# Stage 1 of an attention and feed-forward block: one chunk's statistics ahead, the largest latents read from the values, and an earlier start of TensorE

## The chip, the core and the metric

The kernel runs on one core of a Trainium2 chip. The metric is device time in microseconds from the first to the last instruction of one launch, with the launch's own edges. All data starts and ends in HBM. TensorE has two clock levels, 1.2 and 2.4 GHz, granted by the chip.

## The reference

x is 2 x 2048 tokens of 1024 numbers, in f32. The block computes:

```
n    = layernorm(x)                                # no learned scale
Cq   = n @ Wq_d + bq_d                             # 1024 -> 12
Ckv  = n @ Wkv_d + bkv_d                           # 1024 -> 4, the "latents"
q    = Cq @ W_qk + b_qk                            # 32 heads of 4
p    = softmax(q . Ckv / 2)                        # 32 heads, 2048 x 2048 per batch
V    = Ckv @ Wv_u + bv_u                           # 32 heads of 32
x    = x + (p @ V) @ Wo + bo
x    = x + layernorm(x) @ W.T + bias + the sum over 8 low-rank updates (lora_A, lora_B, lora_weights)
```

Keys and values of all heads are made from the same four latents of a token. So a head's product with the values needs the four latents and a column of ones only, and Wv_u, Wo and the biases are folded into one matrix beforehand.

## The kernel before

The 4096 tokens are 8 chunks of 512 (`CHUNKS`, N = 512), four to a batch (`CB`). Each chunk is four tiles of 128 tokens (`TT`). The code is written out by hand: every engine has its own program, and semaphores are the only thing between them. An engine runs its program strictly in that order, so a wait holds up all that stands behind it.

**Stage 1** makes queries, keys and values of all 8 chunks. For chunk c:
- SyncE loads four tiles of x, 512 KB each (L332), into a ring of four places (`y`, `xn` and two parts of `area`). A place is loaded anew when its chunk has been turned and measured.
- VectorE measures it: `statistics`, eight BATCH_NORM_STATS2 (L1124) and four aggregates (L1201). GpSimd makes 1/sqrt(variance + eps) of it in 14 small operations on 4 columns (L490 to L501) and a diagonal matrix `diag` (L505); TensorE multiplies `diag` with ones (`spread_r`, L705), and ScalarE moves the product to `o_sb` (`move_r`, L590).
- TensorE turns x with the identity, eight `turn_x` of four 128x128 transposes (L678; `turn_first`, L685, for the first half of chunk 0). ScalarE moves each to `x_turned` (`move_turned`, L556). Two `down` (L698) of 32 columns multiply it with `w_down`. The second of chunk c stands in the next chunk's stretch, behind its second `turn_x`.
- VectorE multiplies the result with `o_sb` (`scale_parts`, L1211, into `down_part`). TensorE sums the parts (`sum_parts`, L711), which gives the latents, and makes the queries of `down_part` (`queries`, L727). ScalarE moves the latents twice (`move_latents` L561, `round_latents` L565), TensorE turns them (`turn_latents`, L722), and ScalarE moves these to `c_wide` (`move_values`, L570).
- VectorE takes the largest latent of the chunk (L1225, `c_max`) and splits the latents in bf16 parts, the keys (`split_latents`, L1227 to L1231, into `key_t`). GpSimd splits the queries (`split_q`, L513 to L517), and SyncE stores them (`store_q`, L342, six transfers a chunk, out of two places in turn; `move_q` of chunk c + 2 waits for the store of chunk c).

VectorE's order is: statistics of chunks 0 and 1, then for c from 1 on `scale_parts(c - 1)`, `split_latents(c - 2)`, `statistics(c + 2)`, with `statistics(2)` and `statistics(3)` both behind `scale_parts(0)`.

**The decision.** The softmax has no maximum of its own per row if a bound on the scores is small. Per batch, the largest latents (L735, L1240) weigh the absolute queries (`bounds`, L743); VectorE takes the largest of the result (L1165), TensorE turns it (L792), and VectorE writes `tight` (L1248, L1250). TensorE, ScalarE and SyncE read `tight` and branch; with these inputs the bound is tight and a long part is skipped. The bound also gives a shift that is stored with the queries (`split_shift`, `store_shifts` L362); the first block of queries is then loaded (L369). TensorE runs `keep_busy` beside its waits: transposes whose result nobody reads (L775).

**Stage 2** starts behind it: TensorE makes scores (L903), ScalarE takes 2048 exponentials of 128x1024 (L634), TensorE multiplies them with the values (L914), and the preparation of the weights and the dense layer stand between.

Of the kernel before, what the change touches and what calls it, by code (L numbers as in the profile page):

```python
# [21 lines left out]
F32 = mybir.dt.float32  # L22
# [11 lines left out]
def build_block(nc, x, wq_d, bq_d, w_qk, b_qk, wkv_d, bkv_d, wv_u, bv_u, wo, bo,  # L34
# [38 lines left out]
    with ExitStack() as ctx:  # L73
# [55 lines left out]
        lat = nc.alloc_sbuf_tensor_at("lat", [P, 2, N], F32, offset=probs_at)  # L129
        down_part = nc.alloc_sbuf_tensor_at("down_part", [P, N], F32, offset=probs_at + 4 * 2 * N)  # L130
        part_b = nc.alloc_sbuf_tensor_at("part_b", [P, N], BF16, offset=probs_at + 4 * 3 * N)
        part_high = nc.alloc_sbuf_tensor_at("part_high", [P, 2, N], BF16, offset=probs_at + 4 * 4 * N)
# [13 lines left out]
        c_max = sb("c_max", [P, CHUNKS], F32)  # L146
        c_maxb = sb("c_maxb", [P, B], F32)
# [27 lines left out]
        w_in = sem("w_in")  # L175
        lora_in = sem("lora_in")
# [44 lines left out]
        c_max_ready = sem("c_max_ready")  # L221
# [43 lines left out]
        W_IN = 9 * 16  # L265
# [274 lines left out]
        def _(act):  # L540
# [5 lines left out]
            act.dma_start(bqk_sb[:, 0:1], b_qk.rearrange("(p a) -> p a", a=1)).then_inc(w_in, 16)  # L546
            act.wait_ge(wqk_zero, 2)
            for i in range(4):
                act.dma_start(wqk_sb[32 * i + QROW:32 * i + QROW + QL, :], w_qk).then_inc(w_in, 16)
            act.dma_start(bqk_sb[QROW:QROW + QL, 2:3], bq_d.rearrange("(p a) -> p a", a=1)).then_inc(w_in, 16)  # L550
# [41 lines left out]
            def move_chunk(c):  # L592

                for kb in range(KB):
# [4 lines left out]
                    if kb == KB - 1:  # L599
                        move_r(c)  # L600
# [6 lines left out]
            act.wait_ge(down_ok, 3)  # L607
# [51 lines left out]
        def _(pe):  # L659
            pe.wait_ge(const_ok, 4)  # L660

            def first_weights():
# [4 lines left out]
                nc.tensor.matmul(ps[:, 7, 1:2], wqk_sb[0:32, :], bqk_sb[0:32, 2:3], start=True, stop=True)  # L667
# [3 lines left out]

# [8 lines left out]
            def turn_first():  # L681
                for t in range(TT):
                    pe.wait_ge(x_in[0][t], 16)
                    for kb in range(4):
                        last = nc.tensor.transpose(ps[:, kb, bass.ts(t, P)], x_tiles[0][:, t, bass.ts(kb, P)], ident[:, :])  # L685
                        if t == TT - 1:
                            last.then_inc(t_ready, 1)

            def down(c, four):
# [4 lines left out]
                if c == 0 and four == 0:  # L694
                    pe.wait_ge(down_ok, 4)
# [17 lines left out]
            def turn_latents(c, slot):  # L713
                pe.wait_ge(lat_ready, START + c + 1)

                pe.wait_ge(caug_ready, START + c)
                if c == CHUNKS - 3:
# [11 lines left out]

            def largest(b, bank):  # L730

                pe.wait_ge(c_max_ready, b + 1)
                if b == B - 1:
                    pe.wait_ge(high_ready, CHUNKS)
# [819 lines left out]
```

## Time and profile before

| | us |
|---|---|
| median of 3 runs (lowest, highest) | 2078.73 (2078.69, 2080.83) |
| profiled execution: its time | 2079.62 |
| its span, first to last instruction | 2077.6 |
| ScalarE busy | 1969.5 (95%) |
| of it the 2048 exponentials | 1899.8 |
| TensorE busy | 1962.2 (94%) |
| VectorE busy | 475.6 (23%) |
| GpSimd busy | 214.9 (10%) |
| first exponential starts at | 105.78 |

The shares are of the whole span; stage 1 is its first 106 us, and there the shares are others: each stretch has to be read by itself. The profiled execution's time is 2.0 us above its span and 0.9 us above the median.

### The profile page before, as it was taken

What the parts mean: (1) busy time and instruction counts of PE and PEld (TensorE: products, weight loads), DVE (VectorE), ACT (ScalarE), POOL (GpSimd) and SP (SyncE); (2) the same over time, 40 slices, a digit from 0 to 9 for tenths busy, and PEclk for the clock granted to TensorE, in tenths of its full rate; (3) what the DMA queues carried; (4) which work ended last, traced back from release to release, by engine and by line L of the source; (5) the groups of instructions that cost most, each with busy time, mean ns of one, the idle gap of its engine ahead of it and who ended that gap; (6) DMA issues with size and microseconds to landing.
All of it is one profiled execution on the core that took longest, in us unless ns stands there. A gap on an engine that the chain in (4) does not pass through costs nothing.

```text
span 2077.6 us, 36033 instructions
## 1 busy us (share of the span) xinstructions
PE 1962.2 (94%) x15085; PEld 715.1 (34%) x15085; DVE 475.6 (23%) x1140; ACT 1969.5 (95%) x2185; POOL 214.9 (10%) x220
## 2 busy tenths in 40 slices
PE   7979898999999999999999999999999999999999
PEld 4522222333333333333333333333333333333337
DVE  7713333111121211211121111212111111212115
ACT  5799999999999999999999999999999999999980
POOL 5600000000110002000110001100110001100022
PEclk9999999999999999999999999999999999999999
DMA  8442000000010001000010000100010000100011
GB/s 308 147 137 86 3 26 26 5 25 13 26 35 15 13 26 46 5 13 26 26 35 3 26 25 13 36 15 26 13 46 5 26 13 26 35 15 13 26 41 41
DMA packets 45806, 77.42 MB, mean 37 GB/s; under 512 B 15886, under 2 KB 29766, under 8 KB 45642
## 3 DMA queue, kind: packets, MB, share of 16 engines
q1 hardware_dynamic: 43296, 75.02, 10.7%
q8 instruction: 119, 1.95, 0.4%
q10 hardware_dynamic: 2346, 0.09, 0.1%
q14 instruction: 45, 0.37, 0.1%
HBM read 51.23 MB, written 23.86 MB: 36 GB/s over the span
## 4 chain that ended last, share of the span: by engine, by line
ACT 43%; PE 35%; issue 16%; DVE 0%; DVEq 0%
ACT probs L634 43%; PE ps L914 17%; PE ps L959 10%; PE ps L903 6%; PE ps L948 2%; PE ps L937 0%; PE ps L943 0%; PE ps L775 0%; DVE y L1433 0%; PE ps L1056 0%; PE ps L1052 0%; DVE o_t L1489 0%; ACT o_t L649 0%; ACT o_sb L646 0%; DVE recip L1481 0%
## 5 line engine op out<-in xcount | busy, mean ns | idle before, releaser
L634 ACT ACTIVATE probs<-ps 128x1024 f32<-128x1024 f32 x2048 | 1899.8, 1030 | 17.7 <-PE ps L903 7.1
L914 PE MATMUL ps<-probs,c_wide 128*32 128x512 f32 x8192 | 985.7, 599 | 0.0
L903 PE MATMUL ps<-q_in,key_t 27*128 27x512 bf16 x4096 | 404.2, 385 | 94.1 <-ACT probs L634 90.8
L959 PE MATMUL ps<-w_eff,xn_t 128*128 128x512 f32 x1344 | 394.5, 418 | 0.0
L914 PEld LDWEIGHTS ps<-probs,c_wide 128*32 128x32 f32 x8192 | 212.3, 108 | 424.9 <-issue 220.0
L903 PEld LDWEIGHTS ps<-q_in,key_t 27*128 27x128 bf16 x4096 | 103.0, 91 | 722.7 <-ACT probs L634 715.2
L1433 DVE SCALAR_TENSOR_TENSOR y<-ps,nw,y 128x512 f32<-128x512 f32 x64 | 48.1, 751 | 979.0 <-PE ps L959 967.6
L959 PEld LDWEIGHTS ps<-w_eff,xn_t 128*128 128x128 f32 x1344 | 228.2, 188 | 102.1 <-issue 69.8
L536 POOL TENSOR_TENSOR y<-y,ffn_bias 128x1024 f32<-128x1024 f32 x32 | 76.4, 2388 | 1349.9 <-DVEq L1454 1349.9
L531 POOL TENSOR_TENSOR y<-y,attn_bias 128x1024 f32<-128x1024 f32 x32 | 75.9, 2385 | 463.9 <-DMA y<-in_L_attn_x_dram 463.8
L1417 DVE TENSOR_TENSOR y<-ps,y 128x512 f32<-128x512 f32 x56 | 38.7, 692 | 134.9 <-PE ps L937 134.9
L1184 DVE CAST xn_t<-ps 128x512 fp32r<-128x512 f32 x56 | 38.8, 692 | 123.3 <-PE ps L943 123.3
L937 PE MATMUL ps<-w_vo,o_t 128*128 128x512 f32 x192 | 60.4, 426 | 0.3 <-DVE o_t L1489 0.3
L556 ACT ACTIVATE area<-ps 128x512 f32<-128x512 f32 x64 | 35.3, 616 | 26.4 <-PE ps L678 22.0
L948 PE MATMUL ps<-w_eff,xn_t 128*128 128x512 f32 x192 | 44.7, 391 | 0.0
L943 PE MATMUL ps<-ident,y 128*128 128x128 f32 x256 | 41.0, 285 | 0.1
L1186 DVE TENSOR_TENSOR xn_t<-ps,xn_t 128x512 fp32r<-128x512 f32 x56 | 38.8, 692 | 9.8 <-DVEq L1120 9.8
L1420 DVE BATCH_NORM_STATS2 stats<-y 128x6 f32<-128x512 f32 x56 | 38.9, 695 | 1.9
L948 PEld LDWEIGHTS ps<-w_eff,xn_t 128*128 128x128 f32 x192 | 35.8, 188 | 7.3
L937 PEld LDWEIGHTS ps<-w_vo,o_t 128*128 128x128 f32 x192 | 31.4, 188 | 16.4 <-issue 12.7
L654 ACT ACTIVATE xn_t<-ps 128x512 fp32r<-128x512 f32 x8 | 4.4, 596 | 34.1 <-PE ps L943 34.1
L943 PEld LDWEIGHTS ps<-ident,y 128*128 128x128 f32 x256 | 27.1, 140 | 13.7 <-issue 13.3
(168 smaller groups left out, 619.7 us busy)
## 6 DMA issues: line engine op xcount, KB each, us to landing
y<-in_L_attn_x_dram SPq DMA_DIRECT2D x40, 512.0 KB, 4.3
out_dram<-y SPq DMA_DIRECT2D x31, 512.0 KB, 2.7
area<-in_L_attn_x_dram SPq DMA_DIRECT2D x16, 512.0 KB, 9.1
q_in<-q_parts SPq DMA_DIRECT2D x256, 27.0 KB
q_parts<-q_parts_sb SPq DMA_DIRECT2D x48, 128.0 KB, 2.8
xn<-in_L_attn_x_dram SPq DMA_DIRECT2D x8, 512.0 KB, 7.7
y<-in_L_attn_Wo_dram SPq DMA_DIRECT2D x1, 2048.0 KB, 8.6
xn<-in_L_attn_Wo_dram SPq DMA_DIRECT2D x1, 2048.0 KB, 13.3
```

Of the source, the lines that this page charges most:

```text
L531: pool.tensor_tensor(y[:, t, :], y[:, t, :], attn_bias[:, :], ALU.add).then_inc(xb_ready, 1)
L536: pool.tensor_tensor(y[:, t, :], y[:, t, :], ffn_bias[:, :], ALU.add).then_inc(yb_ready, 1)
L634: nc.scalar.activation(probs[:, (c * STEPS + step) % PROBS, bass.ts(pair, 2 * N)], ps[:, 2 * (i % SCORE_SLOTS):2 * (i % SCORE_SLOTS) + 2, ...
L903: last = nc.tensor.matmul(ps[:, at, :], key_t[TILE * h:TILE * h + KEYS, bass.ts(b * KT + kt, P)], q_in[TILE * h:TILE * h + KEYS, g % 2, :] ...
L914: last = nc.tensor.matmul(ps[32 * h:32 * h + 32, SUMS, :], c_wide[:, b * KT + kt, at:at + 32], probs[:, (c * STEPS + step) % PROBS, bass.t ...
L937: last = nc.tensor.matmul(ps[:, bank, :], o_t[:, a, bass.ts(t, P)], w_vo[:, b, bass.ts(n, N)], start=(i == 0), stop=(i == 2))
L943: last = nc.tensor.transpose(ps[:, bank, bass.ts(a, P)], y[:, t, bass.ts(4 * u + a, P)], ident[:, :])
L948: last = nc.tensor.matmul(ps[:, bank, :], xn_t[:, t % 2, a, kb, :], w_eff[:, b, kb, bass.ts(half, N)], start=(kb + i == 0), stop=(kb == KB ...
L959: last = nc.tensor.matmul(ps[:, SHARED, :], xn_t[:, t % 2, a, kb, :], w_eff[:, b, kb, bass.ts(half, N)], start=(kb + i == 0), stop=(kb == ...
L1184: ch.then(nc.vector.tensor_copy(high, bank_part))
L1420: ch.put(nc.vector.bn_stats(stats[:, t, n, :], y[:, t, bass.ts(n, N)]))
L1433: nc.vector.scalar_tensor_tensor(out=y[:, t, bass.ts(half, N)], in0=ps[:, bank, :], scalar=nw[:, 0, 3, t:t + 1], in1=y[:, t, bass.ts(half, ...
```

## The change

- VectorE: `statistics(c + 1)` instead of `statistics(c + 2)` behind `split_latents(c - 2)`; `split_latents` has no maximum any more. The splits run one per chunk to the end; the last one, of chunk 7, stands behind the instructions that write `tight`.
- The largest latents are taken once per batch from `c_wide`: a maximum over 16 tiles (`largest_of_rows`), a transpose (`turn_largest`), a maximum from PSUM (`largest`).
- TensorE: 16 `keep_busy` transposes ahead of the first tile, and 2, 6 and 4 between the tiles of chunk 0. `spread_r(0)` goes behind the first `down` of the chunk 1 stretch. At the end `turn_latents(7)` stands ahead of `queries(7)`.
- The weights' semaphore is split: the first weights wait for three transfers, not nine; the product with the query bias has its own wait and its own place (`query_bias`).
- ScalarE: `move_r(0)` behind the second `move_turned` of chunk 1, `move_values(7)` ahead of `move_q_abs(7)`; the fourth exponential, not the first, waits for the last keys, and the small buffers are laid elsewhere inside `probs` so that this holds.

```diff
-        lat = nc.alloc_sbuf_tensor_at("lat", [P, 2, N], F32, offset=probs_at)
...
+        part_high = nc.alloc_sbuf_tensor_at("part_high", [P, 2, N], BF16, offset=probs_at + 4 * 7 * N)
+        lat = nc.alloc_sbuf_tensor_at("lat", [P, 2, N], F32, offset=probs_at + 4 * 8 * N)
...
-        W_IN = 9 * 16
+        W_IN = 3 * 16
+        WQK_IN = 6 * 16
...
-                    if kb == KB - 1:
+                    if kb == 1 and c == 1:
+                        move_r(0)
+                    if kb == KB - 1 and c:
                         move_r(c)
...
             move_latents(CHUNKS - 1, 1)
+            move_values(CHUNKS - 1)
             move_q_abs(CHUNKS - 1)
             round_latents(CHUNKS - 1, 1)
-            move_values(CHUNKS - 1)
...
-                        if i == 0:
+                        if i == 3:
                             act.wait_ge(lat_split, START + CHUNKS)
...
+            WARM = (2, 6, 4)
+            keep_busy(16, 5, ident)
...
+                    if t < TT - 1:
+                        keep_busy(WARM[t], 5, ident)
...
+            def turn_largest(b, bank):
+                pe.wait_ge(c_top_ready, b + 1)
+                nc.tensor.transpose(ps[0:L, bank, 0:P], c_top[:, b, :], ident[:, :]).then_inc(c_turned, 1)
...
+            def largest_of_rows(b):
+                dve.wait_ge(caug_ready, START + (b + 1) * CB)
+                nc.vector.tensor_reduce(c_top[:, b, :], c_wide[:, b * KT:(b + 1) * KT, CW:CW + L].rearrange("p t l -> p l t"),
+                                        AX.X, ALU.max, apply_absolute_value=True).then_inc(c_top_ready, 1)
+
+            def largest(b, bank):
+                dve.wait_ge(c_turned, b + 1)
+                nc.vector.tensor_reduce(c_most[:, b:b + 1], ps[0:L, bank, 0:P], AX.X, ALU.max).then_inc(c_most_ready, 1)
...
                 scale_parts(c - 1)
-                if c == 1:
-                    statistics(2)
...
-                if c + 2 < CHUNKS:
-                    statistics(c + 2)
+                if c + 1 < CHUNKS:
+                    statistics(c + 1)
+                if c == CB:
+                    largest_of_rows(0)
...
-            split_latents(CHUNKS - 1, 1, lambda: (largest(1), weigh(1, 5)))
+            largest_of_rows(1)
+            largest(1, 4)
+            weigh(1, 4)
...
-            split_shift(P, 6, shift_split, bound_max[:, 1:2], judge)
+            split_shift(P, 6, shift_split, bound_max[:, 1:2], judge, lambda: split_latents(CHUNKS - 1, 1))
```

How the instructions stand on TensorE at its very start, before (x is in `y`, the turned x in `area`):

```order
L685 MATMUL ps<-ident,y 128x128 x16
L666 MATMUL ps<-ones,small 128x1
L667 MATMUL ps<-bqk_sb,wqk_sb 128x1
L668 MATMUL ps<-w_down,ones 128x256
L678 MATMUL ps<-ident,y 128x128 x8
L698 MATMUL ps<-area,w_down 32x512 x4
L678 MATMUL ps<-ident,y 128x128 x8
L705 MATMUL ps<-diag,ones 128x512
```

And now, with new line numbers (L671 is `keep_busy`, L702 the first tiles, L695 `turn_x`, L717 `down`, L724 `spread_r`):

```order
L671 MATMUL ps<-ident 128x128 x16
L702 MATMUL ps<-ident,y 128x128 x4
L671 MATMUL ps<-ident 128x128 x2
...
L680 MATMUL ps<-ones,small 128x1
L681 MATMUL ps<-w_down,ones 128x256
L695 MATMUL ps<-ident,y 128x128 x4
L688 MATMUL ps<-bqk_sb,wqk_sb 128x1
L695 MATMUL ps<-ident,y 128x128 x4
L717 MATMUL ps<-area,w_down 32x512 x4
L695 MATMUL ps<-ident,y 128x128 x8
L695 MATMUL ps<-ident,xn 128x128 x8
L717 MATMUL ps<-area,w_down 32x512 x4
L724 MATMUL ps<-diag,ones 128x512
```

Twenty-eight transposes are new, the query bias stands between two `turn_x`, and `spread_r(0)` comes two `turn_x` and a `down` later.

VectorE from the measuring of chunk 1 to the second pass of the loop, before:

```order
L1124 BN_STATS stats<-xn 128x6 x8
L1201 BN_AGGR x_mv<-stats 128x2 x4
L1211 TENSOR_TENSOR down_part<-ps,o_sb 128x512
L1124 BN_STATS stats<-area 128x6 x8
L1201 BN_AGGR x_mv<-stats 128x2 x4
L1124 BN_STATS stats<-area 128x6 x8
L1201 BN_AGGR x_mv<-stats 128x2 x4
L1211 TENSOR_TENSOR down_part<-ps,o_sb 128x512
L1225 TENSOR_REDUCE c_max<-lat 128x1
```

And now (L1155 and L1233 measure, L1243 is `scale_parts`, L1254 the first of a split):

```order
L1155 BN_STATS stats<-xn 128x6 x8
L1233 BN_AGGR x_mv<-stats 128x2 x4
L1243 TENSOR_TENSOR down_part<-ps,o_sb 128x512
L1155 BN_STATS stats<-area 128x6 x8
L1233 BN_AGGR x_mv<-stats 128x2 x4
L1243 TENSOR_TENSOR down_part<-ps,o_sb 128x512
L1254 SCALAR_TENSOR_TENSOR part_f<-part_high,less_high,lat 128x512
```

One chunk's measuring is gone from between the first two `scale_parts`, and the maximum from ahead of the split.

VectorE at the decision, before:

```order
L1179 TENSOR_TENSOR shift_parts<-shift_f,shift_parts 128x512
L1222 TENSOR_REDUCE c_max<-lat 128x1
L1236 TENSOR_REDUCE c_maxb<-c_max 128x1
L1240 TENSOR_SCALAR bound_w<-head_of_row,ps 128x32
L1227 SCALAR_TENSOR_TENSOR part_f<-part_high,less_high,lat 128x512
L1229 CAST part_b<-part_f 128x512
L1231 SCALAR_TENSOR_TENSOR key_t<-part_b,less_high,part_f 128x512
L1165 TENSOR_REDUCE bound_max<-ps 128x1
```

And now, up to the writing of `tight` and what follows it:

```order
L1211 TENSOR_TENSOR shift_parts<-shift_f,shift_parts 128x512
L1264 TENSOR_REDUCE c_top<-c_wide 128x4
L1269 TENSOR_REDUCE c_most<-ps 4x1
L1273 TENSOR_SCALAR bound_w<-head_of_row,ps 128x32
L1196 TENSOR_REDUCE bound_max<-ps 128x1
L1278 TENSOR_REDUCE bound_max<-bound_max 128x1
L1281 TENSOR_REDUCE tight_f<-ps 1x1
L1283 TENSOR_SCALAR tight<-tight_f 1x1
L1199 TENSOR_SCALAR shift_f<-ps 128x512
L1254 SCALAR_TENSOR_TENSOR part_f<-part_high,less_high,lat 128x512
```

The three instructions of the split went from ahead of the bound's maximum to behind `tight`.

## Rows read from the trace of the kernel before

**Rows 1.** Page, part 5: busy, mean ns | idle before, releaser.
```profile
L634 ACT ACTIVATE probs<-ps 128x1024 f32<-128x1024 f32 x2048 | 1899.8, 1030 | 17.7 <-PE ps L903 7.1
```

**Rows 2.** Waits, 0 to 106 us: waiter <- releaser: us in total, times, longest.
```profile
ACT probs L634 <- PE ps L903: 6.3, 1, 6.3
DVE less_high L1273 <- DMA bqk_sb<-in_L_attn_bq_d_dram: 2.3, 1, 2.3
```

**Rows 3.** Windows: length, busy PE, PEld, DVE, ACT, POOL, PE clock, DMA.
```profile
16.00:18.00 2.00, 1.45 (x8) 0.23 (x8) 2.00 (x5) 0.53 (x1) 1.46 (x7) 1.00 1.03 412
50.00:60.00 10.00, 9.39 (x63) 5.39 (x60) 9.33 (x18) 8.00 (x17) 7.74 (x19) 1.00 0.85 291
108.00:109.00 1.00, 1.00 (x9) 0.67 (x7) 0.00 (x0) 1.00 (x2) 0.00 (x0) 0.50 0.32 33
```

**Rows 4.** Timeline, TensorE, 0 to 112 us: start, us, line, tiles, [idle before].
```profile
6.11 2.30 PE L685 MATMUL ps<-ident,y 128*128 128x128 f32 x8 [6.11 <-DMA y<-in_L_attn_x_dram]
10.75 1.11 PE L685 MATMUL ps<-ident,y 128*128 128x128 f32 x4 [0.19 <-DMA y<-in_L_attn_x_dram]
16.55 1.93 PE L698 MATMUL ps<-area,w_down 128*32 128x512 f32 x8 [0.66 <-ACT area L556]
18.42 1.97 PE L678 MATMUL ps<-ident,y 128*128 128x128 f32 x8
20.30 1.96 PE L705 MATMUL ps<-diag,ones 128*128 128x512 f32 x2
22.10 1.04 PE L678 MATMUL ps<-ident,xn 128*128 128x128 f32 x8
25.53 1.12 PE L711 MATMUL ps<-down_part,spread 128*128 128x512 f32 x2 [0.38 <-DVE down_part L1211]
37.41 1.12 PE L711 MATMUL ps<-down_part,spread 128*128 128x512 f32 x2 [2.81 <-DVE down_part L1211]
76.87 1.12 PE L711 MATMUL ps<-down_part,spread 128*128 128x512 f32 x2 [0.86 <-DVE down_part L1211]
86.92 1.02 PE L711 MATMUL ps<-down_part,spread 128*128 128x512 f32 x2
94.97 1.12 PE L711 MATMUL ps<-down_part,spread 128*128 128x512 f32 x2 [0.18 <-DVE down_part L1211]
```

**Rows 5.** Timeline, VectorE, 0 to 112 us.
```profile
16.32 4.84 DVE L1124 BATCH_NORM_STATS2 stats<-xn 128x6 f32<-128x512 f32 x8
56.79 0.68 DVE L1225 TENSOR_REDUCE c_max<-lat 128x1 f32<-128x512 f32 x1
57.38 1.61 DVE L1227 SCALAR_TENSOR_TENSOR part_f<-part_high,less_high,lat 128x512 f32<-128x512 bf16 x1
```

**Rows 6.** Timeline, GpSimd, 50 to 112 us.
```profile
58.53 0.54 POOL L490 TENSOR_SCALAR x_r<-x_mv 128x4 f32<-128x4 f32 x1
63.31 1.04 POOL L505 TENSOR_TENSOR diag<-ident,x_r 128x512 f32<-128x512 f32 x1
66.96 1.16 POOL L517 TENSOR_TENSOR q_parts_sb<-part_f,q_parts_sb 128x512 bf16<-128x512 f32 x1
```

**Rows 7.** Timeline, VectorE, TensorE and ScalarE at the decision.
```profile
98.80 0.25 DVE L1240 TENSOR_SCALAR bound_w<-head_of_row,ps 128x32 f32<-128x32 f32 x1 [0.93 <-PE ps L735]
99.18 1.07 PE L743 MATMUL ps<-q_abs,bound_w 128*32 128x512 f32 x8
102.02 0.68 DVE L1165 TENSOR_REDUCE bound_max<-ps 128x1 f32<-128x512 f32 x1
103.81 0.14 DVE L1250 TENSOR_SCALAR tight<-tight_f 1x1 int32<-1x1 f32 x1 [0.18 <-DVEq L1120]
105.78 5.77 ACT L634 ACTIVATE probs<-ps 128x1024 f32<-128x1024 f32 x6 [6.29 <-PE ps L903]
```

**Rows 8.** Timeline, SyncE's queue, 0 to 130 us.
```profile
48.63 4.49 SPq L342 DMA_DIRECT2D q_parts<-q_parts_sb  x6
99.33 2.81 SPq L369 DMA_DIRECT2D q_in<-q_parts  x8
```

More of the change, by code:

```diff
@@ L175, in build_block @@
         w_in = sem("w_in")
+        wqk_in = sem("wqk_in")
+        query_ps = sem("query_ps")
         lora_in = sem("lora_in")
@@ L660, in _, with keep_busy @@
             pe.wait_ge(const_ok, 4)
+            def keep_busy(times, bank, tile=wqk_sb):
+                for _ in range(times):
+                    nc.tensor.transpose(ps[:, bank, 0:P], tile[:, :], ident[:, :])
+            WARM = (2, 6, 4)
+            keep_busy(16, 5, ident)
             def first_weights():
@@ L670, in first_weights, with query_bias @@
                 last.then_inc(bias_ps, 1)
+            def query_bias():
+                pe.wait_ge(wqk_in, WQK_IN)
+                nc.tensor.matmul(ps[:, 6, 0:1], wqk_sb[0:32, :], bqk_sb[0:32, 2:3], start=True, stop=True).then_inc(query_ps, 1)
             def turn_x(c, kb):
@@ L716, in turn_latents @@
                 pe.wait_ge(caug_ready, START + c)
+                if c == 0:
+                    pe.wait_ge(down_ok, 4)
+                if c == CHUNKS - 4:
+                    pe.wait_ge(c_most_ready, 1)
                 if c == CHUNKS - 3:
@@ L756, in stage1 @@
                         down(c - 1, 1)
+                    if kb == 1 and c == 1:
+                        spread_r(0)
+                    if kb == 2 and c == CHUNKS - 3:
+                        pe.wait_ge(caug_ready, START + c - 1)
+                        turn_largest(0, 6)
                     if kb == 2 and c == CHUNKS - 2:
@@ L764, in stage1 @@
                         sum_parts(c - 1)
+                    if kb == 4 and c == 0:
+                        query_bias()
                     if kb == 5:
@@ L769, in stage1 @@
                         queries(c - 1)
-                    if kb == KB - 1:
+                    if kb == KB - 1 and c:
                         spread_r(c)
-            def keep_busy(times, bank):
-                for _ in range(times):
-                    nc.tensor.transpose(ps[:, bank, 0:P], wqk_sb[:, :], ident[:, :])
             for c in range(CHUNKS):
@@ L791, in _ @@
             pe.wait_ge(min_ready, 1)
-            nc.tensor.matmul(ps[0:1, 4, 0:P], bound_max[:, B:B + 1], ident[:, :], start=True, stop=True).then_inc(tight_ps, 1)
+            nc.tensor.matmul(ps[0:1, 4, 2 * P:3 * P], bound_max[:, B:B + 1], ident[:, :], start=True, stop=True).then_inc(tight_ps, 1)
             keep_busy(4, 0)
+            pe.wait_ge(high_ready, CHUNKS)
             pe.wait_ge(tight_ok, 1)
@@ L1170, in split_shift @@
                 if then:
+                    beside()
                     dve.wait_ge(first_shift, SHIFT_BLOCKS * 16)
@@ L1174, in split_shift @@
                 ch.then(nc.vector.tensor_tensor(rest, shift, parts[:, 0, :], ALU.subtract))
-                if beside:
+                if beside and not then:
                     beside()
@@ L1211, in scale_parts, with split_latents @@
                 nc.vector.tensor_tensor(down_part[:, :], ps[:, 4, :], o_sb[:, :], ALU.mult).then_inc(part_ready, 1)
-            def split_latents(c, slot, meanwhile=None):
+            def split_latents(c, slot):
                 ch = Chain(v_lat)
@@ L1220, in split_latents @@
                 rest = part_f[:, 0, :]
-                if meanwhile:
-                    ch.then(nc.vector.tensor_reduce(c_max[:, bass.ds(c, 1)], src, AX.X, ALU.max, apply_absolute_value=True))
-                    meanwhile()
-                else:
-                    ch.put(nc.vector.tensor_reduce(c_max[:, bass.ds(c, 1)], src, AX.X, ALU.max, apply_absolute_value=True))
                 dve.wait_ge(high_ready, c + 1)
@@ L1247, in judge @@
                 ch = Chain(v_set)
-                ch.then(nc.vector.tensor_reduce(tight_f[:, :], ps[0:1, 4, 0:P], AX.X, ALU.max))
+                ch.then(nc.vector.tensor_reduce(tight_f[:, :], ps[0:1, 4, 2 * P:3 * P], AX.X, ALU.max))
                 ch.end()
```

53 lines of the change are left out of this document (25 added, 28 removed).

## The prediction

> **What bounds the kernel now.** I read the page's costliest groups first. The 2048 exponentials on ScalarE take 1899.8 us, 1030 ns each, and ScalarE is idle only 17.7 us in all ahead of them [rows 1]. So from the first exponential to the end ScalarE is the bound, and none of its work is changed. The waits of the first 106 us then show that 6.3 us of those 17.7 are the wait for the very first scores [rows 2], and the timeline has the first exponential at 105.78 [rows 7]. This change can move that 105.78 and nothing behind it. The profiled execution took 2079.62 us, 0.9 more than the median of the runs; I do the sum on it and take 0.9 off.
>
> Stage 1 has stretches with different bounds. The marks are the starts of `sum_parts` (L711) on TensorE [rows 4]: chunk 0 at 25.53, chunk 1 at 37.41, chunk 5 at 76.87, chunk 6 at 86.92, chunk 7 at 94.97. Between chunks 1 and 5 a chunk takes 39.46 / 4 = 9.87 us, and the window there has VectorE busy 9.33 of 10, TensorE 9.39 (pipelined, so no proof of a bound), ScalarE 8.0, GpSimd 7.7 [rows 3]. TensorE waits for VectorE's `down_part` each time, 0.86 us at chunk 5 and 2.81 at chunk 1 [rows 4]. VectorE sets this stretch. Between chunks 5 and 6 it has nothing to measure, and the pace is 10.05, of which 1.07 is the bounds' product, whose like is in rows 7: TensorE alone needs 9.0 a chunk.
>
> The start is slow for another reason. Eight transposes take 1.97 us at 18.42 and 1.04 at 22.10; the product at 20.30 takes 1.96, twice its later 1.02 to 1.12 [rows 4]. So TensorE ran at its lower level, 1.2 GHz, up to about 22 us, after which it ran at 2.4. The clock column says 1.00 from 16 to 18 us [rows 3], which the durations do not bear out; I go by them. At 108 us the column says 0.50 after a pause of TensorE ahead of the first scores [rows 3].
>
> **Part 1, the start.** Sixteen transposes now fill TensorE from GpSimd's last constants, a little over 2 us, to the first tile, which it now awaits idle until 6.11 [rows 4]: at 1.97 / 8 = 0.25 us they take 3.9 us, in time that was idle. Twelve more lie between the tiles, whose arrival sets the pace (the fourth is turned at 10.75, right after its DMA [rows 4]). If the clock is still low they cost: 16 + 12 transposes from 6.1 on take 6.9 us and end at about 13.0 rather than 11.9. If it rises on the way, they end with the last tile, at 11.3. I take it that it rises by about 9 us, since TensorE then has no gap from 2 us on, as it had none from 18.42 on ahead of the rise at 22.
> The wait for weights costs VectorE 2.3 us, released by the ninth of nine small transfers [rows 2]. The first three are enough now. VectorE then measures the fourth tile as it comes (a tile is a quarter of 4.84 us [rows 5]): 10.75 + 1.25 + 0.45 for aggregates = 12.5. TensorE has the weight sums at 12.5, VectorE centres `w_down` in 1.1 us more, and the first `down` starts at 14.0, where it was 16.55 [rows 4]. At 1.04 for two `turn_x` or one `down`: two `turn_x` to 16.0, chunk 1's first two to 17.1 (its last tile lands at 10.75 + 4 x 1.28 = 15.9, 512 KB at the 412 GB/s of [rows 3]), `down` to 18.1. `diag` takes GpSimd 5.8 us from the measured tiles (58.53 to 64.35 [rows 6]): 12.7 + 5.8 = 18.5. `spread_r(0)` ends at 19.5, its move 0.6 later. VectorE meanwhile measures chunk 1 from 14.1 to 19.5. All three meet at 20: `scale_parts(0)` starts at 20.0 and `sum_parts(0)` at 20.75, 4.8 earlier than before.
>
> By the Trainium skill, page "TensorE: Matmul & The Clock Gate", section "Part 4: PE-mode transpose", transposes do not count as TensorE work for the clock in the way that matmuls do. By that rule 28 transposes would not lift the clock, and the sum loses the 4.8 us and some more; the trace leaves it open, since the stretch from 18.42 to 22 is half transposes and half products. It is the first rival below.
>
> **Part 2, chunk 1.** Between the first two `scale_parts` VectorE had two chunks to measure, 2 x 5.3 us; now it has one, and it is done 5.9 us after 20.0, before TensorE is. TensorE's own 9.05 a chunk decides: `sum_parts(1)` at 29.8, before 37.41. That is 7.6 earlier, 2.8 of it new.
>
> **Part 3, chunks 1 to 5.** The maximum goes: 0.59 us from its start to the next instruction [rows 5]. VectorE's pace becomes 9.87 - 0.59 = 9.28. What is late next: TensorE at 9.0, and GpSimd, whose pass from L490 at 58.53 to the end of L517 at 68.12 holds 0.7 of waiting [rows 6], so 8.9. Two loops are new or tighter. (a) `diag` of the next chunk is wanted 5.9 us after `scale_parts`, and GpSimd gets the numbers 0.2 before it: 5.6 against 5.9. Written as a loop over two chunks it is 8.9 + 0.2 + 5.8 + 3.1 = 18.0, or 9.0 a chunk. (b) Behind that GpSimd splits queries one chunk later than before, 3.1 us, then come six stores (4.49 us of SyncE [rows 8]) and their landing, about 2.4, and `move_q` two chunks on waits for them: 8.9 a chunk by the same count. Five things stand between 8.9 and 9.3. Bounds: 9.05, and 9.87 if nothing is won. I take 9.3, VectorE's own. `sum_parts(5)` at 29.8 + 37.2 = 67.0; the gain is 9.9. The new small maxima and transpose (0.3 us or less each, once per batch) lie inside that rounding.
>
> **Part 4, chunks 5 to 7.** TensorE's order is the same but for one small product; VectorE now measures chunk 7 here, where it was idle. Cost 0, up to 0.5 if its pass of 9.3 comes against TensorE's 10.05. `sum_parts(7)` at 67.0 + 18.1 = 85.1.
>
> **Part 5, the decision.** Before, the weights `bound_w` start 3.83 us after `sum_parts(7)`, the product stands from 99.18 to 100.25, and its maximum starts at 102.02 only, because VectorE is still splitting the last latents [rows 7]. That 1.77 of delay goes. Against it stands a longer way to `bound_w`: latents moved, turned, moved to the values, maximum, transpose, maximum, product, and TensorE does the queries' product (1.0) before that transpose. With steps of 0.3 to 0.7 I come to 4.6 rather than 3.83, product to 6.05, maximum at 6.1 rather than 7.05: 0.95 saved, bounds 0 and 1.7. From that maximum to the first exponential it stays 3.76 [rows 7]. The last split now lies beside the first three exponentials (3.1 us against 3.8 from `tight` on, less the 1.8 in which ScalarE waits anyway): cost 0. The first queries are loaded 4.36 us after `sum_parts(7)` [rows 8]; SyncE must first have stored chunk 5, which is split a pass later than before, and there I count up to 1.6 us of delay against about 1.5 of slack. I take 0.2.
>
> **Sum.** First exponential at 85.1 + 6.1 + 3.76 + 0.2 = 95.2, before 105.78: 10.6 us. 2079.62 - 10.6 = 2069.0, and on the median's scale **2068.1**. Best: pace 9.05 (1.0), no 0.2, decision 0.4 better: 2066.5. Worst with the clock up: pace 9.87 (2.3), decision half: 2071.5. That is this case's own range.
>
> **Rivals.**
> *The clock stays low until about 22 us or later.* For it: no row shows a rise after transposes alone. Against: the stretch before the rise at 22 was half transposes. Then the twelve extra transposes push everything by 1.1 us, `spread_r(0)` stands behind two `turn_x` and a `down` at 1.9 each, and `sum_parts(0)` comes at 25.5 to 28, where it was 25.53. The rest of the gain, 5.8, stays, less 0 to 2.5: 2073 to 2075.4, middle 2074.2.
> *The new loops bind.* GpSimd's operations and VectorE's splits now lie side by side; the split's first instruction took 1.61 us beside GpSimd [rows 5], and GpSimd's first 0.54 [rows 6]. At a pace of 10.1: 5 x 0.8 = 4 more, 2072.1.
> *Slower.* One mechanism: `diag` late in every pass. TensorE is strictly in order, and behind `spread_r` stand all transposes of the next chunk, for which ScalarE waits, then `down`, then VectorE. Loop (a) at 18.0 has to grow to 23.8 before six passes lose 6 x 2.6 = 15.6 against my pace and the kernel comes to 2083.7; it breaks even at a pace of 11.1, with 10 us rather than 5.8 for `diag`. For it: the slack is only 0.3 us. Against: even a full 1 us of overlap makes 9.5.
> *The gain is lost at the end*: queries late, or a hold-up at the branch, so that the start's 10 us shrink below 4: 2077 to 2079. Nothing in the rows speaks for so much.
>
> **Chances.** Forecast 0.68, low clock 0.18, loops 0.08, slower 0.04, lost 0.02. The range 2066.3 to 2074.4 leaves out half of the low clock, the slower and the lost, and the forecast's tails. No change means within 0.2%, or 4.2 us, about what a measurement of this kernel can tell: faster means below 2074.6. That is 0.68 + 0.08 + 0.11 of the low clock = 0.87; same 0.07 + 0.02 = 0.09; slower 0.04.
>
> **What would show it.** First exponential at 95. Transposes of chunk 0 from about 9 us at the later duration (1.04 for eight), `scale_parts(0)` at 20. `sum_parts` starts 9.1 to 9.4 apart from chunk 1 to 5, with waits below 0.4 ahead of them. The bound's maximum right behind its product. The same 1900 us of exponentials, with no new wait at the fourth. I am wrong if transposes last 1.97 for eight up to 20 us, if TensorE or its weight load is shown waiting for `diag`, if ScalarE waits for stores ahead of the queries, or if scores wait for `q_in`.

## The result, and the profile after

Faster, by less than half of what I forecast: the median is 2074.99 us (2073.84 to 2076.40, 10 runs) against 2079.26 (2077.44 to 2080.83, 10 runs of the kernel before), a ratio of 0.9979 with a 95% interval of 0.9970 to 0.9987. That is 4.3 us, where the forecast was 10.6, and the time lies 0.6 us above the range. The profiled execution took 2074.25 us, its span 2072.5. It is 5.4 us below the profiled execution of before, where the medians are 4.3 apart: what follows explains the profiles, and about 1 us of their distance is spread between executions.

The page again has the exponentials first, line, tiles, busy, mean and idle time ahead; it answers to [rows 1]:

```profile
L641 ACT ACTIVATE probs<-ps 128x1024 f32<-128x1024 f32 x2048 | 1899.9, 1030 | 19.4 <-PE ps L934 8.8
```

The work is the same, and the idle time ahead of it is 19.4 us, which was 17.7. The first exponential starts at 100.50, 5.28 earlier than 105.78 [rows 7]; from it to the last instruction it is 1971.96 us, before 1971.87. So in these two profiles the whole difference is in stage 1 and the decision, and 5.3 us are missing there. The marks are the eight `sum_parts` (L730 now) on TensorE's timeline: start, us, line, tiles, idle before. They answer to [rows 4].

```profile
21.29 1.12 PE L730 MATMUL ps<-down_part,spread 128*128 128x512 f32 x2 [1.05 <-DVE down_part L1243]
30.33 1.12 PE L730 MATMUL ps<-down_part,spread 128*128 128x512 f32 x2
57.45 1.13 PE L730 MATMUL ps<-down_part,spread 128*128 128x512 f32 x2
66.86 1.02 PE L730 MATMUL ps<-down_part,spread 128*128 128x512 f32 x2
78.41 1.02 PE L730 MATMUL ps<-down_part,spread 128*128 128x512 f32 x2
86.61 1.13 PE L730 MATMUL ps<-down_part,spread 128*128 128x512 f32 x2 [0.32 <-DVE down_part L1243]
```

Up to chunk 5 the gain is 76.87 - 66.86 = 10.0 us, as forecast (67.0). At chunk 7 it is 94.97 - 86.61 = 8.4, at the first exponential 5.3. Two places gave it back. The first is ScalarE's wait between chunks 5 and 6 (timeline):

```profile
66.44 0.69 ACT L586 ACTIVATE q_parts_sb<-ps,bqk_sb 128x512 bf16<-128x512 f32 x1 [2.06 <-DMA q_parts<-q_parts_sb]
```

`move_q(4)`, which writes the queries of chunk 4 into the place that the store of chunk 2 reads, waited 2.06 us for that store, and all that stands behind it on ScalarE moved back; the chunk took 11.55 us (66.86 to 78.41), before 10.05. SyncE's queue shows what was issued ahead of that store:

```profile
51.17 1.97 SPq L337 DMA_DIRECT2D area<-in_L_attn_x_dram  x4
...
53.90 0.76 SPq L356 DMA_DIRECT2D small<-_L_ffn_lora_weights_dram  x1
54.71 0.45 SPq L358 DMA_DIRECT2D attn_bias<-in_L_attn_bo_dram  x1
55.20 0.73 SPq L359 DMA_DIRECT2D ffn_bias<-in_L_ffn_bias_dram  x1
55.97 0.45 SPq L360 DMA_DIRECT2D lora_a_sb<-in_L_ffn_lora_A_dram  x1
56.46 9.63 SPq L347 DMA_DIRECT2D q_parts<-q_parts_sb  x7
```

Chunk 7 of x (2 MB) and 1.5 MB of weights and biases that nobody needs before stage 2. The store's packets, issued from 56.46 on, moved between 62.5 and 65.5 us only, and its last landing is told at 66.42.

The second place is the decision. The four instructions that mark it, on VectorE, TensorE and ScalarE (timeline, against [rows 7]):

```profile
92.52 0.69 DVE L1196 TENSOR_REDUCE bound_max<-ps 128x1 f32<-128x512 f32 x1 [1.29 <-PE ps L768]
94.66 0.14 DVE L1283 TENSOR_SCALAR tight<-tight_f 1x1 int32<-1x1 f32 x1 [0.18 <-DVEq L1151]
99.86 0.61 PE L934 MATMUL ps<-q_in,key_t 27*128 27x512 bf16 x4 [5.10 <-issue]
100.50 1.94 ACT L641 ACTIVATE probs<-ps 128x1024 f32<-128x1024 f32 x2 [7.96 <-PE ps L934]
```

```profile
L827 PEldq COMPARE_BRANCH  x1: 3979/3979/3979, 95.8 to 95.8; - x1
L796 PEldq COMPARE_BRANCH  x1: 365/365/365, 104.9 to 104.9; - x1
```

It took 3.98 us, before 0.37. Inside it, from 97.42 to 98.30, comes one transfer of 16 KB on the queue that the page calls "instruction", and the branch ends 1.50 us behind that. The program up to the branch is 1174 instructions long on TensorE, before 1108: the change put 66 more ahead of it.

The window from 95 us on shows something else (columns as in [rows 3]): TensorE stood idle, and the granted clock is 0.62 on average; it was at the lower level from 96.88 to 103.70, 6.8 us. In the profile of before it was there too, for 3.4 us from 107.35 on.

```profile
95.00:104.00 9.00, 4.14 (x23) 2.94 (x24) 4.57 (x8) 2.99 (x4) 0.75 (x1) 0.62 0.47 65
```

### The profile page after: what moved, and what is told of

The parts are those of the page before. It is cut to its first block, busy times and chain, and to the rows that moved or that the text cites. A ratio compares the mean times of both kernels' runs of the same rounds, so it can differ in the third digit from the quotient of the medians.

```text
span 2072.5 us, 36094 instructions
## 1 busy us (share of the span) xinstructions
PE 1962.6 (95%) x15118; PEld 718.0 (35%) x15118; DVE 469.7 (23%) x1134; ACT 1969.4 (95%) x2185; POOL 215.2 (10%) x220
## 3 DMA queue, kind: packets, MB, share of 16 engines
q8 instruction: 120, 1.97, 0.4%
## 4 chain that ended last, share of the span: by engine, by line
ACT 36%; PE 35%; issue 13%; DVE 0%; DVEq 0%
ACT probs L641 36%; PE ps L945 17%; PE ps L990 10%; PE ps L934 6%; PE ps L979 2%; PE ps L968 0%; PE ps L974 0%; DVE y L1467 0%; DVE w_eff L1218 0%; PE ps L899 0%; PE ps L1087 0%; PE ps L1083 0%; DVE o_t L1523 0%; ACT o_t L656 0%; ACT o_sb L653 0%
## 5 line engine op out<-in xcount | busy, mean ns | idle before, releaser
L641 ACT ACTIVATE probs<-ps 128x1024 f32<-128x1024 f32 x2048 | 1899.9, 1030 | 19.4 <-PE ps L934 8.8
```

The lines of the kernel that those rows point to most:

```text
L641: nc.scalar.activation(probs[:, (c * STEPS + step) % PROBS, bass.ts(pair, 2 * N)], ps[:, 2 * (i % SCORE_SLOTS):2 * (i % SCORE_SLOTS) + 2, ...
```

## Experiments

Theory A: the branch is slow because its target is not loaded yet, and that hangs on how many instructions stand ahead of it. Rival B: it is slow because TensorE stood idle, or because of the wait put ahead of it. Theory C: the 2.06 us come from the loads ahead of the store. Beside these, each part of the forecast got a run.

**More instructions ahead of the branch, in the changed kernel (e1).**

```diff
+            for _ in range(40):
+                pe.sem_inc(padding, 1)
             pe.wait_ge(const_ok, 4)
...
             keep_busy(16, 5, ident)
+            for _ in range(60):
+                pe.sem_inc(padding, 1)
```

> The changed kernel with 100 more instructions on TensorE ahead of the branch (semaphore increments that nobody waits for, 40 before the first transposes, 60 behind the 16), nothing else. Theory A (the branch on TensorE waited for its instructions: its compare-and-branch took 3.98 us against 0.37 before, with one 16 KB instruction load inside it, because the 66 instructions that the change adds ahead of the branch moved its target out of the part already loaded): the 5th load of 16 KB comes ahead of the branch, the branch takes 0.3 to 0.5 us, scores start 1.3 us behind tight rather than 5.1, and the time falls by 3 to 4 us to about 2071. Theory B (the scores waited for q_in or for something else behind the branch): the branch or the wait stays as long as before, time 2075.

Measured 2081.33 us (ratio 1.0013, 1.0003 to 1.0022), from 2078.29 to 2086.76, and the branch 3.62 us in a profile of 2085.78. A failed as I had put it: the fifth load did not come ahead of the branch but at 107.21, 0.94 behind its start. So the count does not work as simply as I thought. As a measure of the time the run is of no use: each increment took TensorE 0.154 us, and `sum_parts(0)` slipped by 9 us to 30.14. That the branch is as slow in the quickest of its executions is not shown.

**The kernel before with 66 increments more, so that its branch stands where the changed one has it (e2).**

```diff
+            for _ in range(66):
+                pe.sem_inc(padding, 1)
             pe.wait_ge(const_ok, 4)
```

> The kernel before with 66 semaphore increments on TensorE ahead of its first transposes, so that its branch stands at the same place in the program as the changed kernel's. Theory A: its branch takes about 4 us rather than 0.37 and the kernel is 3.5 us slower than before, with nothing else changed. Theory B: no change, within 0.5 us.

Measured 2083.76 us (1.0023, 1.0014 to 1.0032). The branch took 3.78 us instead of 0.37. The rows of its timeline at the decision:

```profile
102.78 0.14 DVE L1253 TENSOR_SCALAR tight<-tight_f 1x1 int32<-1x1 f32 x1 [0.18 <-DVEq L1123]
107.66 0.61 PE L906 MATMUL ps<-q_in,key_t 27*128 27x512 bf16 x4 [4.78 <-issue]
108.37 1.94 ACT L635 ACTIVATE probs<-ps 128x1024 f32<-128x1024 f32 x2 [9.90 <-PE ps L906]
```

The scores come 4.88 us behind `tight`, in the kernel before, with none of the changed waits. So the number of instructions ahead decides, as A has it, and of B the added wait falls. The rest of the kernel did not stay as it was: TensorE began at 11.01, and `tight` comes 1.0 earlier than before; behind the first exponential it is 1973.57 us, 1.7 more than before, with two falls of the clock where before has one.

**The changed kernel without its 28 transposes, with 56 increments in their place (e3).**

```diff
+            for _ in range(56):
+                pe.sem_inc(padding, 1)
             pe.wait_ge(const_ok, 4)
...
-            keep_busy(16, 5, ident)
...
-                    if t < TT - 1:
-                        keep_busy(WARM[t], 5, ident)
```

> The changed kernel without its 28 new transposes at the start, with 56 semaphore increments in their place so that the branch stays where it is. If these transposes lift the clock: without them eight transposes take 1.9 us until about 20 us, sum_parts(0) starts at 24.5 to 26 rather than 21.3, and the time is 3 to 5 us above the changed kernel. If the early start comes from the weights' semaphore and the order alone: within 1 us of the changed kernel.

Measured 2076.53 us (0.9987, 0.9978 to 0.9996). `sum_parts(0)` came at 22.00, 0.7 later, and the clock rose at 12.4 instead of 8.1. By this run the transposes would be worth less than I had thought; but the increments changed the start as well. TensorE started at 9.51 here, behind the increments, when most of chunk 0 had landed, and had no gap from then on:

```profile
9.51 3.33 PE L704 MATMUL ps<-ident,y 128*128 128x128 f32 x16 [9.51 <-issue]
```

**The changed kernel with the five loads (L355 to L360) behind the store of chunk 2 (e4).**

```diff
             load_tiles(RING + 3)
+            store_q(2, 0)
             sp.dma_start(bv_rows, bv_u.rearrange("(g p) -> g p", p=P)).then_inc(lora_in, 16)
...
-            for c in range(2, CHUNKS - 4):
-                store_q(c, c % 2)
+            store_q(3, 1)
```

> The changed kernel with the five loads of biases and low-rank weights (1.5 MB, needed in stage 2 only) issued behind the store of chunk 2 and not ahead of it. Theory C (the 2.06 us in which ScalarE waited for the store of chunk 2 ahead of the queries of chunk 4 comes from these loads and x of chunk 7 standing ahead of that store in the DMA queues): the wait goes or falls below 0.5 us, chunk 5 to chunk 6 takes 10.1 us rather than 11.55, the first exponential comes 1.4 us earlier, time 1.0 to 1.6 below the changed kernel. Rival: the wait is the latency of the loop over two chunks (split, six issues, landing) whatever stands in the queue, and stays above 1.5 us.

Measured 2072.96 us (0.9968, 0.9955 to 0.9980), 2.0 less than the changed kernel. ScalarE's `move_q(4)` now starts with no wait, and chunk 6 comes 9.95 us after chunk 5:

```profile
63.96 0.69 ACT L586 ACTIVATE q_parts_sb<-ps,bqk_sb 128x512 bf16<-128x512 f32 x1
...
66.55 1.02 PE L730 MATMUL ps<-down_part,spread 128*128 128x512 f32 x2
76.50 1.02 PE L730 MATMUL ps<-down_part,spread 128*128 128x512 f32 x2
```

That is theory C: the store now lands at 61.99, 6.0 us behind its issue instead of 10.0. A wait of 0.9 us for a store is left ahead of `move_q(7)`. The gain is more than the 1.0 to 1.6 us that I had expected.

**Fewer instructions ahead of the branch, the filling kept (e5).** Nearly the same time on TensorE in few wide products (behind the branch the transposes stay):

```diff
-                for _ in range(times):
-                    nc.tensor.transpose(ps[:, bank, 0:P], tile[:, :], ident[:, :])
+                for n in {16: (4, 4), 12: (3, 3)}.get(times, ((times + 1) // 2,)):
+                    nc.tensor.matmul(ps[:, bank, 0:n * P].rearrange("p (k m) -> p k m", m=P), ones[:, :],
+                                     ones[:, :].unsqueeze(1).to_broadcast([P, n, P]), start=True, stop=True)
```

> The changed kernel with its filling transposes ahead of the branch replaced by few wide f32 products of ones by ones that keep TensorE busy about as long (16 transposes: 2 products of 512 columns; 6 or 5: one of 384; 12: two of 384; 4: one of 256; 2: one of 128). TensorE's program up to the branch is 70 instructions shorter, 1104 instead of 1174 (before: 1108). Theory A (the branch takes 4 us because its target is not yet loaded when that many instructions stand ahead of it): the branch takes 0.4 us, the scores begin 1.4 us after tight instead of 5.05, first exponential at 96.8 to 97.2, time 2071.2 to 2071.6 (3.5 us less than the changed kernel). Rival B (the branch is slow because TensorE stood idle, or because of the wait ahead of it, not because of the count): branch at 3.3 to 4.0 us as in the changed kernel and time 2074 to 2076.

Measured 2069.63 us (0.9957, 0.9943 to 0.9971): 5.4 less than the changed kernel, where I had expected 3.5.

```profile
L832 PEldq COMPARE_BRANCH  x1: 362/362/362, 95.9 to 95.9; - x1
94.79 0.14 DVE L1288 TENSOR_SCALAR tight<-tight_f 1x1 int32<-1x1 f32 x1 [0.18 <-DVEq L1156]
96.35 0.40 PE L939 MATMUL ps<-q_in,key_t 27*128 27x512 bf16 x4 [1.43 <-issue]
96.78 16.70 ACT L641 ACTIVATE probs<-ps 128x1024 f32<-128x1024 f32 x18 [4.13 <-PE ps L939]
```

The branch took 0.36 us, the scores come 1.56 behind `tight`, and a group of 18 exponentials has no gap in it, where the changed kernel had one after two. The 16 KB of instructions were loaded at 97.40 here too, but nobody waited for them. TensorE's idle time and the wait ahead of the branch are as in the changed kernel, so the rest of B falls too. The first exponential is 3.72 us earlier. The other 1.1 us of this profile lie behind it: from the first exponential to the end it is 1970.84 us and not 1971.96, and here the clock did not fall. That second cost is not the branch's alone. The profile of the kernel before, whose branch is quick, has a fall and 1971.87 us, and that of e10, with the same quick branch and the same code behind it, has no fall and 1970.89. So a fall goes with about 1.1 us more whatever the branch did. Near the decision there was one in all six profiles with a slow branch, and in one of the six with a quick one.

**Both cures together (e6): fewer instructions, later loads.**

> The same, and with the five loads of biases and LoRA weights (1.5 MB) issued behind the store of chunk 2. Theory A and theory C (the store of chunk 2 stands behind these loads) are independent of each other, so both gains should add: first exponential at 97.79 less 3.0 to 3.5, that is 94.3 to 94.8, time 2069.0 to 2069.8. If the two share one cause (a queue held up), the time is that of the better one alone, 2071 to 2073.

Measured 2068.00 us (2067.56 to 2068.56; ratio 0.9945, 0.9931 to 0.9958). It is the best version of this study, 7.0 us below the changed kernel and 11.5 below the one before.

```profile
66.81 1.02 PE L735 MATMUL ps<-down_part,spread 128*128 128x512 f32 x2
...
84.81 1.13 PE L735 MATMUL ps<-down_part,spread 128*128 128x512 f32 x2
...
91.70 2.81 SPq L374 DMA_DIRECT2D q_in<-q_parts  x8
...
92.89 0.14 DVE L1288 TENSOR_SCALAR tight<-tight_f 1x1 int32<-1x1 f32 x1 [0.18 <-DVEq L1156]
94.78 0.39 PE L939 MATMUL ps<-q_in,key_t 27*128 27x512 bf16 x4 [1.75 <-DMA q_in<-q_parts]
95.21 18.58 ACT L641 ACTIVATE probs<-ps 128x1024 f32<-128x1024 f32 x20 [3.46 <-PE ps L939]
```

The time is 1.0 us below the range that I expected and the first exponential 0.4 us behind it: I had counted from the profile of e4. Chunk 7 gains 1.90 against e5, the first exponential 1.57, because the scores now wait for `q_in`, the first queries: the next limit. The same window as in the changed kernel shows the clock at 1.00 throughout.

```profile
95.00:104.00 9.00, 7.38 (x68) 3.03 (x64) 3.22 (x6) 8.79 (x10) 0.00 (x0) 1.00 0.42 65
```

**The changed kernel without its 28 transposes, nothing in their place (e7).** The edit is that of e3 without the increments; the branch stands at 1118.

> The changed kernel without the 28 transposes at its start and with nothing in their place: the branch stands at instruction 1118. If TensorE's clock needs them, it rises 8 to 14 us later (12 to 22) and sum_parts(0) comes at 22.0 to 25; by the run with pauses in their place it rises at about 12.4 and costs 0.7 to 1.5 us at sum_parts(0). The branch: theory A says 0.4 us if the target is loaded with 1118 as with 1108, else 3.3 to 4.0. With a fast branch and the clock 1 us late: first exponential at 97.5 to 98.5, time 2072 to 2073; with a slow branch 2075.5 to 2077.

Measured 2072.77 us (0.9965, 0.9951 to 0.9979): 2.2 faster than the changed kernel, although it lacks the warm start. The branch took 0.36 us. The start, where TensorE's clock rose at 16.7:

```profile
6.16 1.08 PE L701 MATMUL ps<-ident,y 128*128 128x128 f32 x4 [6.16 <-DMA y<-in_L_attn_x_dram]
...
9.84 1.12 PE L701 MATMUL ps<-ident,y 128*128 128x128 f32 x4 [1.28 <-DMA y<-in_L_attn_x_dram]
...
15.30 1.12 PE L694 MATMUL ps<-ident,y 128*128 128x128 f32 x4
17.49 1.09 PE L694 MATMUL ps<-ident,y 128*128 128x128 f32 x8
23.44 1.12 PE L727 MATMUL ps<-down_part,spread 128*128 128x512 f32 x2 [1.05 <-DVE down_part L1240]
```

Four transposes take as long up to 15.30 as eight from 17.49 on. Against e5, which has a warm start and a fast branch as well, `sum_parts(0)` is 2.2 us late (23.44 to 21.23), and so is the first exponential (99.03 to 96.78): that is what the warm start is worth. It is more than I had expected from e3. The medians are 3.1 apart; the rest, in the profile, goes with a fall of the clock at 2013.5 us, far from the edit, that came in some kernels' profiles and not in others. In the changed kernel the 56 instructions of the warm start cost more at the branch than they won.

**The changed kernel with the old order of the statistics (e8).**

```diff
                 scale_parts(c - 1)
+                if c == 1:
+                    statistics(2)
...
-                if c + 1 < CHUNKS:
-                    statistics(c + 1)
+                if c + 2 < CHUNKS:
+                    statistics(c + 2)
```

> The changed kernel with the order of the statistics undone: statistics(2) ahead of the first split again, then two chunks ahead. If this part of the change carried the steps that the prediction gave it: sum_parts(1) comes 4.2 to 5.5 us later (34 to 36 instead of 30.33), the pace from there is the old 9.7 or so, sum_parts(5) at 72 to 74 instead of 66.86, time 2079 to 2081. Rival: the pace is set by ScalarE and the diagonal's way now, and only the first chunk pays: sum_parts(1) late by 4 to 5 us, the pace 9.0 to 9.3, time 2077 to 2079. Rival: TensorE's early clock alone gave the better pace, and the order of the statistics nothing: sum_parts(1) within 1 us of 30.33, time 2074 to 2076.

Measured 2078.43 us (0.9993, 0.9984 to 1.0002): without this part 3.4 of the changed kernel's 4.3 us are gone.

```profile
21.49 1.13 PE L730 MATMUL ps<-down_part,spread 128*128 128x512 f32 x2 [1.04 <-DVE down_part L1243]
33.37 1.12 PE L730 MATMUL ps<-down_part,spread 128*128 128x512 f32 x2 [2.81 <-DVE down_part L1243]
...
70.95 1.12 PE L730 MATMUL ps<-down_part,spread 128*128 128x512 f32 x2
81.00 1.02 PE L730 MATMUL ps<-down_part,spread 128*128 128x512 f32 x2
```

Chunk 1 comes 3.04 later with the 2.81 of waiting of [rows 4], the pace from there to chunk 5 is (70.95 - 33.37) / 4 = 9.40 rather than (66.86 - 30.33) / 4 = 9.13, and chunk 5 comes 4.1 later. My expectation had 72 to 74 for it; it is 70.95, probably since the maximum of each chunk (0.59 us) stays out: the pace of before was 9.87. From 5 to 6 it takes 10.05, with no wait for a store, and chunk 7 is only 2.8 late. The store of chunk 2 lands as late as ever, 10.5 us behind its issue, but it is issued 4.9 us behind `move_q(2)` and not 10.3 as in the changed kernel: with the old order the queries are split a chunk earlier, and `move_q(4)` comes 3.2 us behind the landing. The first exponential is 2.6 later than in the changed kernel (103.06); the rest of the 3.4 goes with the clock, which fell twice in this profile.

**The split of the last keys ahead of the bound's maximum again, on e6 (e9).**

```diff
             weigh(1, 4)
+            split_latents(CHUNKS - 1, 1)
             dve.wait_ge(shift_split, 1)
```

(and not between the instructions behind `tight`.)

> The short branch and the later loads kept (the version of 2068.00 us), and the split of the last keys put ahead of the bound's maximum again, as before the change. The bound's maximum stands at 90.72 there, with VectorE free from 89.44; the split is 1.6 + 0.45 + 0.85 = 2.9 us long and ends at 92.4 at the earliest. If the maximum sets the end: tight at 94.6 to 94.9, scores 1.2 later at 95.8 to 96.1 instead of 94.77, first exponential 1.0 to 1.4 later, time 2069.0 to 2069.5. Rival: the queries' transfer (scores waited for q_in at 94.77) covers the whole of it: first exponential within 0.2 us, time 2067.8 to 2068.3.

Measured 2068.80 us (2068.53 to 2069.01), 0.8 above e6.

```profile
91.96 0.68 DVE L1201 TENSOR_REDUCE bound_max<-ps 128x1 f32<-128x512 f32 x1
93.76 0.14 DVE L1288 TENSOR_SCALAR tight<-tight_f 1x1 int32<-1x1 f32 x1 [0.18 <-DVEq L1156]
95.34 0.39 PE L939 MATMUL ps<-q_in,key_t 27*128 27x512 bf16 x4 [1.45 <-DMA q_in<-q_parts]
```

Neither expectation is met in full. Its `sum_parts(7)` is at 84.98, so the maximum comes 6.98 behind it and not 5.91 as in e6: 1.07 later. `tight` is only 0.70 later, and the scores, which wait for `q_in` either way, 0.40. The profile shows 0.56 at the first exponential, the medians 0.8.

**The kernel before with the later loads (e10).**

> The kernel before, with the five loads of biases and LoRA weights behind the store of chunk 2, and nothing else. In its trace no instruction of ScalarE waited for that store, since its chunks are 0.7 us longer each. If the hold-up is new with the change (theory C): no gain, sum_parts(5), (6), (7) within 0.3 us of 76.87, 86.92, 94.98, time 2079 to 2080 (ratio 0.999 to 1.001). Rival (the loads took bandwidth from the chunks of x before too): sum_parts(7) earlier by 1 us or more, time 2077.5 to 2078.5.

Measured 2080.09 us (1.0001, 0.9992 to 1.0010): no change. The store lands at 64.88, 5.8 us behind its issue, where it was 9.7 in the kernel before (58.47 to 68.20); but there `move_q(4)` came at 73.54, 5.3 us behind the landing. So the loads made the store late before as well and held up nothing; the change used up the slack.

## Why the prediction was wrong

**Part 1, the start: right, 0.5 us late.** `scale_parts(0)` came at 20.55 (20.0), `sum_parts(0)` at 21.29 (20.75). The clock rose at 8.1; TensorE had had nothing but transposes from 2.24 on. Their durations show it, sixteen in 3.67 at first and then four in 0.60:

```profile
2.24 3.67 PE L671 MATMUL ps<-ident 128*128 128x128 f32 x16 [2.24 <-POOL spread L484]
...
9.99 0.60 PE L671 MATMUL ps<-ident 128*128 128x128 f32 x4
```

So the first rival is out. The Trainium skill's page "TensorE: Matmul & The Clock Gate", section "Part 4: PE-mode transpose", has transposes not counted as work for the clock; this trace disagrees, with the rise at 8.1, and the measurement decides. What I had not asked is what the transposes are worth if the rule is wrong: e7 against e5 says 2.2 us at `sum_parts(0)`. The rest of the 4.2 us gained there (25.53 to 21.29) must be the shorter wait for weights and the new order of `spread_r` and `move_r`; no run here parted these two.

**Part 2, chunk 1: right.** `sum_parts(1)` at 30.33 (29.8), the whole difference from Part 1; e8 takes 3.04 of it back, where I had said 2.8.

**Part 3, the pace: right on the mark, by a wrong bound.** I took VectorE's 9.28. The chunks came 9.04 apart up to the fifth `sum_parts` and 9.41 once, with the new transpose and small product in it. TensorE sets it, as far as the profile tells: the marks of chunks 1 to 5 have no wait ahead of them, and the window shows it full, against [rows 3]:

```profile
50.00:60.00 10.00, 10.00 (x71) 5.66 (x69) 8.94 (x20) 8.63 (x17) 8.50 (x20) 1.00 0.92 321
```

`sum_parts(5)` at 66.86 (67.0). The loops (a) and (b) of GpSimd did not bind up to here.

**Part 4, chunks 5 to 7: wrong, 19.75 us for 18.1.** I had called this stretch unchanged. The term that was too small stands in loop (b) of Part 3: six stores of 4.49 us and "their landing, about 2.4", 6.9 in all. For the store of chunk 2 it was 10.0 (56.46 to 66.42), because it stood behind 3.5 MB of loads, and ScalarE waited 2.06. It was 9.7 in the kernel before too. What changed is the slack: the split of the queries comes one chunk later, as loop (b) has it, so the store is issued 10.3 us behind `move_q(2)` rather than 4.4, and a slack of 5.3 us at `move_q(4)` is gone. With the old order it is still 3.2 (e8), so the order took most of it and the quicker pace little. In e6, with the store ahead of 1.5 MB of the loads, the stretch takes 84.81 - 66.81 = 18.0. The list of what would prove me wrong had "if ScalarE waits for stores".

**Part 5, the decision: right up to the maximum.** It starts 5.91 behind `sum_parts(7)` (6.1), right behind its product. Then `tight` took 2.14 and not 1.79, since TensorE's product with `bound_max` now stood behind the twelve filling transposes: 0.35 of the forecast's 3.76. The last split lies beside the branch and the scores, with no new wait at the fourth exponential. e9 gives the moved split 0.4 us at the scores and 0.8 in the medians, within the bounds of 0 and 1.7.

**From `tight` on: the step that failed.** "From that maximum to the first exponential it stays 3.76" was 7.98. The branch cost 3.6 us more, and the other 0.25 went largely to the scores at the low clock (0.61 for 0.39). The sum of what is missing: 1.51 at `sum_parts(7)`, less 0.19 in the decision, 0.35 at `tight`, 3.87 from `tight` on, less my 0.2 for queries: 5.34, and 100.50 - 95.16 is 5.34. I had this as the last rival, "a hold-up at the branch", at 0.02, and said that nothing in the rows spoke for it. None did: the rows of before show a quick branch. But the change adds 66 instructions to TensorE ahead of it, and I priced them only by their time on the array. That they change where the program stands when the jump comes was not in my list of costs. (One bound was also added up wrong: the two terms named for the worst, 2.3 and 0.5, give 2070.9 and not 2071.5. The argument does not rest on it.)

With both hold-ups out (e6) the first exponential starts at 95.21, where the forecast had 95.2, and the time is 2068.00, where it had 2068.1. That is luck in good part. The first exponential is 0.5 late at the start, 0.7 better in the pace and 0.2 up to the maximum, and 0.5 late again behind it, where the scores wait for `q_in`, one of my signs of being wrong. And the time: from the first exponential to the end e6 takes 1970.85 us and not 1971.87, since its clock did not fall. The sum has no such term; on the other side its base of 2078.73 is 0.5 to 0.8 below the kernel before beside these runs. The whole gain of e6 is 11.5 us, not 10.6.

What stays open: where between 1118 and 1174 instructions the branch turns slow, and how the length decides it. Shown are the two sides: 1104, 1108 and 1118 fast, 1174 (in both kernels, with transposes or increments) and 1274 slow. That the slow branch waits for the 16 KB of instructions is argued, from its end 1.3 to 1.5 us behind that transfer in all six slow profiles; no run took the transfer away.

## What to carry to other kernels

An instruction put in idle time is not free if a jump over code comes behind it: count instructions as well as microseconds, look at the branch's own record, and fill a wait with few wide operations rather than many small ones. When a stretch gets faster, ask of each transfer how far it stands behind others in its queue, not how long it takes alone, and how long its reader can wait: a store that had 5.3 us of slack held up ScalarE once its data were made a chunk later, behind loads whose first use in the profile is 90 us on. And when two terms of a sum come out right and the time does not, undo the suspected hold-ups one by one and then together, and compare every mark of the sum: a total that comes back can hide errors that cancel.

## What the runs showed of the hardware

- A taken branch on TensorE took 0.36 to 0.37 us in the kernel before, e5, e6, e7, e9 and e10, and 3.3 to 4.0 us in the changed kernel, e1 to e4 and e8. In all twelve profiles one transfer of 16 KB on the instruction queue begins 0.9 to 1.6 us after the branch's start; the slow branches end 1.3 to 1.5 us behind the end of that transfer, the quick ones before it begins.
- A semaphore increment costs TensorE's instruction stream 0.15 us: the first work begins at 9.51 behind 56 of them and at 11.01 behind 66.
- With nothing on TensorE but f32 transposes from 2.24 us on, its clock rose to 2.4 GHz at 8.1. With the same start it rose at 6.2 in e4 and at 11.8 in e8, which cost 0.2 us only; with products in place of the added transposes at 6.7, 8.2 and 8.2 (e5, e6, e9).
- TensorE's clock fell to the lower level for 6.8 us, beginning inside each slow branch, with TensorE idle, and for 3.4 us behind the quick branch of the kernel before, but not near that of e5, e6, e7, e9 and e10.
- From the first exponential to the end it is 1970.8 to 1971.0 us in the profiles without a fall of the clock ahead of the last 3 us (e5, e6, e9, e10), 1971.9 to 1972.1 with one (before, changed, e3, e7) and 1973.4 to 1973.8 with two (e1, e2, e4, e8).
- The 768 KB store of chunk 2 landed 9.3 to 10.5 us after its first issue behind 3.5 MB of loads (before, changed, e1 to e3, e5, e7, e8) and 5.8 to 7.2 us behind the 2 MB of x alone (e4, e6, e9, e10).
